# Second mixer's queries and maxima laid out by DMA, first mixer re-spaced

## The reference

```python
x = x + mixer_a(layernorm(x))   # linear attention, 32 heads of 4, two decays per head, rotary positions
x = x + ffn(layernorm(x))       # sum over 8 experts of (silu(x @ Wg) * (x @ Wu)) @ Wd, 128 -> 512 -> 128
x = x + mixer_b(layernorm(x))   # causal softmax attention, 16 query heads of 8, one key and one value head
x = x + ffn(layernorm(x))       # the same experts
```

## Time and profile before

| | |
|---|---|
| time, median of 3 runs | 1625.97 us (1619.76 to 1626.56) |
| profiled execution | 1626.03 us, span 1624.0 us |
| TensorE (PE) busy | 1496.0 us, 92% of the span |
| VectorE (DVE) busy | 1177.7 us, 73% |
| ScalarE (ACT) busy | 885.3 us, 55% |
| GpSimd (POOL) busy | 784.3 us, 48% |
| DMA | 216.28 MB, 133 GB/s over the span |
| granted TensorE clock | 0.976 of full speed |

### The profile page before, as it was taken

The page is one execution under the profiler, slowest core; times in us unless marked ns, Lnnn a source line. Parts: engine busy times, 40 slices in busy tenths (PEclk is TensorE's granted clock), DMA queues, the critical chain, the costliest instruction groups (busy, mean ns, idle before and its releaser), DMA issues. The chain is left out here.

```text
span 1624.0 us, 23328 instructions
## 1 busy us (share of the span) xinstructions
PE 1496.0 (92%) x7504; PEld 1111.4 (68%) x7504; DVE 1177.7 (73%) x1949; ACT 885.3 (55%) x1520; POOL 784.3 (48%) x732
## 2 busy tenths in 40 slices
PE   3478999899989899899999999999999999999998
PEld 2356777677776677577567676776767767677786
DVE  5678787869778787868677585775857758577565
ACT  2245556464554546444655557565575655755554
POOL 2537445543525244531315546555465554655565
PEclk8689999999999999999999999999999999999999
DMA  6125543434334343433332334333343333433352
GB/s 202 59 71 179 198 154 119 156 117 156 140 133 156 117 156 117 156 117 117 117 133 101 118 117 150 123 131 117 119 156 121 125 117 122 156 119 124 148 182 112
DMA packets 36380, 216.28 MB, mean 133 GB/s; under 512 B 3491, under 2 KB 17444, under 8 KB 19876
## 3 DMA queue, kind: packets, MB, share of 16 engines
q1 hardware_dynamic: 36260, 214.79, 36.5%
HBM read 200.10 MB, written 15.27 MB: 133 GB/s over the span
## 5 line engine op out<-in xcount | busy, mean ns | idle before, releaser
L531 POOL TENSOR_TENSOR HL<-HF,HH 128x512 fp32r<-128x512 f32 x312 | 416.0, 1333 | 476.4 <-ACT HH L705 475.3
L1215 DVE TENSOR_TENSOR HF<-SG,bank 128x512 f32<-128x512 f32 x512 | 350.4, 684 | 171.8 <-PE bank L874 92.1
L872 PE MATMUL bank<-XTH,W 128*128 128x512 f32 x1024 | 423.4, 413 | 10.4 <-ACT SG L698 9.9
L874 PE MATMUL bank<-XTH,W 128*128 128x512 f32 x1024 | 403.8, 394 | 0.0
L873 PE MATMUL bank<-XTL,W 128*128 128x512 f32 x1024 | 403.6, 394 | 0.0
L1198 DVE SCALAR_TENSOR_TENSOR SG<-SG,bank 128x512 f32<-128x512 f32 x288 | 197.3, 685 | 207.0 <-ACT SG L700 205.0
L700 ACT ACTIVATE SG<-bank 128x512 f32<-128x512 f32 x288 | 172.1, 597 | 318.0 <-PE bank L874 316.5
L705 ACT ACTIVATE HH<-HF 128x512 fp32r<-128x512 f32 x512 | 320.4, 626 | 37.6 <-DVE HF L1215 32.4
L698 ACT ACTIVATE SG<-bank 128x512 f32<-128x512 f32 x224 | 133.5, 596 | 251.7 <-PE bank L874 250.4
L872 PEld LDWEIGHTS bank<-XTH,W 128*128 128x128 f32 x1024 | 194.4, 190 | 82.3 <-issue 23.6
L872 PE MATMUL dbank<-HH,W 128*128 128x512 f32 x512 | 217.9, 426 | 16.1 <-DVE HL L1204 14.9
(11 more groups left out here) (212 smaller groups left out, 1796.7 us busy)
## 6 DMA issues: line engine op xcount, KB each, us to landing
W<-kept_w SPq DMA_DIRECT2D x120, 1536.0 KB, 6.3
kept_w<-W SPq DMA_DIRECT2D x8, 1536.0 KB, 6.2
X<-in_L_attn_a_x_dram SPq DMA_DIRECT2D x8, 256.0 KB, 5.7
WS<-in_L_ffn_Wg_dram SPq DMA_DIRECT2D x8, 256.0 KB, 6.4
WS<-in_L_ffn_Wu_dram SPq DMA_DIRECT2D x8, 256.0 KB, 6.7
WS<-in_L_ffn_Wd_dram SPq DMA_DIRECT2D x8, 256.0 KB, 6.5
out_dram<-X SPq DMA_DIRECT2D x8, 256.0 KB, 7.2
CST<-in_tables_dram SPq DMA_DIRECT2D x1, 834.0 KB, 6.4
```

The lines of the kernel that those rows point to most:

```text
L531: g.tensor_tensor(HL[:, n % HRING, :], HF[:, n % HFRING, :], HH[:, n % HRING, :].bitcast(F32), ALU.subtract).then_inc(F.hl, 1)
L872: pe.matmul(dst, wh, xh, start=start, stop=False)
L874: return pe.matmul(dst, wl, xh, start=False, stop=stop)
L1215: v.tensor_tensor(HF[:, n % HFRING, :], gated, fbank[(2 * n + 1) % 3], ALU.mult).then_inc(F.mul, 1)
```

## The change

Second mixer: the 0/1 matrices, `query_stack` and `stack2` go. SyncE stores QKH and QKL of the queries to HBM and loads them back spread over QST; VectorE splits the maxima into a small tile NMS, TensorE transposes it, ScalarE copies it (MT), SyncE stores it and loads it into the free partitions of QST. The maxima of a sequence are stored at r = 8 and 14 and spread at r = 9 and 15. `rows` then uses 24 of each 32 partitions, `cols` 26. The weight loads become part of a SyncE list by slots. Projections move three slots earlier, each of the column scores has its own slot, `exps` stands ahead of the gate's activation in its slot, and the buffer of exponentials is a ring.

First mixer: v2 and rep0 swap banks; Relu moves from ScalarE to GpSimd; the last two scans, the products that use them, the second numerators and all that follows come one slot later; in stages 0 to 5 the gate of unit 28 uses Tanh, as in the last stage, so that ScalarE keeps the table of Exp (`AHEAD`). `GAP` is 3 instead of 4, `B_LEAD` 35 instead of 36.

```diff
+AHEAD = [UNIT * s + 28 for s in range(NT - 2)]
-GAP = 4
+GAP = 3
-B_LEAD = 36
+B_LEAD = 35
...
-          "b1": (-6, 2, 2), "mx": (-5, 1, 0), "v0": (1, 1, 0), "den": (3, 2, 1), "v1": (4, 1, 0), "v2": (6, 0, 0),
-          "rep0": (6, 1, 1), "rep1": (7, 1, 2), "v3": (8, 1, 0), "z": (20, 2, 2), "fturn": (31, 1, 2)}
-NUM_POINT = ((13, 1), (17, 1))
+          "b1": (-6, 2, 2), "mx": (-5, 1, 0), "v0": (1, 1, 0), "den": (3, 2, 1), "v1": (4, 1, 0), "v2": (6, 0, 1),
+          "rep0": (6, 1, 0), "rep1": (7, 1, 2), "v3": (8, 1, 0), "z": (21, 2, 2), "fturn": (32, 1, 2)}
+NUM_POINT = ((13, 1), (18, 1))
+B_CELL = {"turn": (-17, 1, 3), "q": (-11, 2, 0), "qs": (-10, 1, 1), "k": (-10, 2, 2), "ks": (-9, 1, 0),
+          "v": (-8, 1, 1), ("mx", 0): (8, 1, 3), ("mx", 1): (14, 1, 3), ("pv", 0, 0): (17, 1, 3),
...
-COLS_AT = [[(12, 2), (14, 0), (15, 2), (17, 0)], [(18, 2), (20, 0), (21, 2), (23, 0)]]
+COLS_AT = [[(12, 2), (13, 2), (14, 2), (15, 2)], [(17, 2), (18, 2), (19, 2), (20, 2)]]
...
+            def spread_queries(t, part, src, done):
+                for g in range(NG):
+                    to = RG * g + DB * part
+                    rows = kept_q[src, RG * g:RG * (g + 1), :].rearrange("(j x) t -> x j t", j=NJ)
+                    sp.dma_start(QST[to:to + DB, :, :].bitcast(F32), rows).then_inc(done, 16)
+            def spread_maxima(n, b):
+                sp.wait_ge(B.mt_out, 32 * (n + 1))
+                rows = kept_m[b].rearrange("(r g j) t -> g r j t", r=2, g=NG)
+                for g in range(NG):
+                    to = RG * g + 3 * DB
+                    sp.dma_start(QST[to:to + 2, :, b * SEQ:(b + 1) * SEQ].bitcast(F32),
+                                 rows[g]).then_inc(B.mrow, 16)
+            def side_b(t, r):
+                if r == -8:
+                    sp.wait_ge(B.hi, 2 * t + 1)
+                    sp.dma_start(kept_q[0], QKH[:, 0, :].bitcast(F32)).then_inc(B.hi_out, 16)
+                if r == -7:
+                    sp.wait_ge(B.lo, 2 * t + 1)
+                    sp.dma_start(kept_q[1], QKL[:, 0, :].bitcast(F32)).then_inc(B.lo_out, 16)
+                    sp.wait_ge(B.hi_out, 16 * (t + 1))
+                    spread_queries(t, 0, 0, B.st_hi)
+                    spread_queries(t, 1, 0, B.st_hi)
+                if r == -6:
+                    sp.wait_ge(B.lo_out, 16 * (t + 1))
+                    spread_queries(t, 2, 1, B.st_lo)
...
+            for slot in range(0, G_LAST + 1):
+                for t, r in b_tiles(slot):
+                    side_b(t, r)
+                for x in range(NE, 2 * NT * NE):
+                    u = FC * (x - WRING + 1) - 1
+                    if slot == ffn_slot(u // UNIT) + u % UNIT + LAG + 1:
+                        load_weights(x)
...
+                if r in (-5, -3):                              # GpSimd, first mixer
+                    k = (r + 5) // 2
+                    g.wait_ge((A.u_k, A.u_q)[k], t + 1)
+                    g.tensor_scalar(R1[:, k, :], U[:, k, :], 0.0, None, ALU.max).then_inc(A.re, 1)
...
+            def gated_ahead(n):                                # VectorE
+                gated = SG[:, n % 2, :]
+                v.wait_ge(F.sil, n + 1)
+                v.scalar_tensor_tensor(gated, gated, 1.0, fbank[2 * n % 3], ALU.add,
+                                       ALU.mult).then_inc(F.mid, 1)
...
-                for (m, c), at in zip(SCANS, (0, 1, 3, 6, 8, 10, 12, 13, 14, 15)):
+                for (m, c), at in zip(SCANS, (0, 1, 3, 6, 8, 10, 12, 13, 15, 16)):
```

More of the change, by code:

```diff
@@ L308, in program @@
         Y = here("Y", u_at, TOK)
-        Z = here("Z", u_at + 4 * TOK, SUB, C)
-        ZN = here("ZN", u_at + 8 * TOK, SUB, C)
+        Z = take("Z", SUB, C)
+        ZN = take("ZN", SUB, C)
         PQ = take("PQ", TOK)
@@ L327, in program @@
         at["now"] = arena
-        NMP = take("NMP", 2, 2, NJ, P, dt=F32R)
+        NMS = take("NMS", 2, 64, dt=F32R)
+        MT = take("MT", 2, P, dt=F32R)
         VF = take("VF", SUB, RG)
         at["now"] = s_at
+        B1 = take("B1", 2, TOK)
+        B2 = take("B2", 2, TOK)
+        QK = take("QK", 2, TOK)
         QKH = take("QKH", 2, TOK, dt=F32R)
@@ L334, in program @@
         KST = take("KST", TOK, dt=F32R)
[L335 to L339, removed]
+        assert at["now"] <= r_at
+        PT = take("PT", 3 * PT_RING, TOK)
         OS = take("OS", 2, TOK)
@@ L355, in program @@
                       "rs ay y xb z zsum zg zb done")
-        B = sems("b", "proj roped u_q u_k hi lo v_ready v_used st_ready st_used kst_used row_ready row_used nmh nml "
-                      "q2_ready q2_used t_ready t_used t_cut pv os turn ro o ot otc out biased done")
-        F = sems("f", "gate up sil half mul hh hl hlv down ys back done")
+        B = sems("b", "proj roped u_q u_k hi lo v_ready v_used hi_out lo_out st_hi st_lo kst_used row_ready row_used nmh nml "
+                      "mx mt mt_out mrow t_ready t_used t_cut pv os turn ro o ot otc out biased done")
+        F = sems("f", "gate up sil half mul hh hl hlv down ys back done mid")
         stored = sem("stored")
@@ L393, in a_tiles @@
         def a_tiles(g):
-            return tiles(g, a_slot, -15, 32)
+            return tiles(g, a_slot, -15, 33)
         def b_tiles(g):
@@ L497, in _, with load_weights @@
             sp.dma_start(BRAW[:, C:], row(b_bk)).then_inc(ld.wb, 16)
-            for x in range(NE, 2 * NT * NE):
+            def load_weights(x):
                 sp.wait_ge(F.down, FC * (x - WRING + 1))
@@ new lines, in _ @@
+            for slot in range(0, G_LAST + 1):
[5 more added lines that the diff above has]
+                        load_weights(x)
+                        if x % NE == 4 and x // NE > NT:
+                            t = x // NE - NT - 1
+                            sp.wait_ge(F.done, NT + t + 1)
+                            sp.dma_start(o_tok[:, t], X[:, t, :, :]).then_inc(stored, 16)
@@ L696, in gate_act @@
                 after(act, F.mul, n - 1)
-                if n < TANH:
+                if n < TANH and n not in AHEAD:
                     act.activation(SG[:, n % 2, :], fbank[2 * n % 3], ACT.Silu).then_inc(F.sil, 1)
@@ L757, in side_a @@
                     act.activation(EX[:, :, :], U[:, :, :], ACT.Exp).then_inc(A.ex, 1)
-                if r == -2:
-                    act.wait_ge(A.ex, t + 1)
-                    act.activation(U[:, :, :], U[:, :, :], ACT.Relu).then_inc(A.re, 1)
                 if r in (7, 8):
@@ L810, in side_b @@
                             act.activation(OS[:, z, :], abank, ACT.Copy).then_inc(B.os, 1)
-                    for h in range(2):
-                        if r == B_CELL["stack", b, h][0]:
-                            act.wait_ge(B.q2_ready, 2 * n + h + 1)
-                            after(act, B.t_ready, 4 * (n - 1))
-                            act.activation(Q2[:, b, 2 * h:2 * h + 2, :], r3(sbank[bank_of(("b", t, ("stack", b, h)))], 2),
-                                           ACT.Copy).then_inc(B.q2_used, 1)
+                    if r == B_CELL["mx", b][0]:
+                        act.wait_ge(B.mx, n + 1)
+                        after(act, B.mt_out, 32 * (n - 1))
+                        act.activation(MT[0:64, b, :], sbank[bank_of(("b", t, ("mx", b)))][0:64, 0:P],
+                                       ACT.Copy).then_inc(B.mt, 1)
                     if r == B_CELL["ot", b][0]:
@@ L840, in _ @@
                 n = unit_of(slot)
-                if n is not None:
-                    gate_act(n)
+                if slot == b_slot(0):
+                    act.wait_ge(A.done, NT)
+                    act.wait_ge(A.z, NT)
                 for t, r in b_tiles(slot):
@@ L845, in _ @@
                         for i, (at, point) in enumerate(COLS_AT[b]):
-                            if r == at + (point == 2):
+                            if r == at + 1:
                                 exps(SPT * t + b, i)
+                if n is not None:
+                    gate_act(n)
                 n = unit_of(slot - 1)
@@ L996, in rows @@
                     pe.wait_ge(B.kst_used, t + 1)
-                    pe.wait_ge(B.st_used, NJ * (t + 1))
-                q = [QST[g * RG:(g + 1) * RG, :, b * SEQ:(b + 1) * SEQ] for g in range(NG)]
-                ks = [KST[g * RG:(g + 1) * RG, b * SEQ:(b + 1) * SEQ] for g in range(NG)]
+                    pe.wait_ge(B.st_hi, 8 * 16 * (t + 1))
+                    pe.wait_ge(B.st_lo, 4 * 16 * (t + 1))
+                q = [QST[g * RG:g * RG + 3 * DB, :, b * SEQ:(b + 1) * SEQ] for g in range(NG)]
+                ks = [KST[g * RG:g * RG + 3 * DB, b * SEQ:(b + 1) * SEQ] for g in range(NG)]
                 masks(i)
@@ L1056, in project_out, with turn_maxima @@
                 m.then_inc(B.out, 1)
-            def stack2(n, b, h, bk):
-                pe.wait_ge(B.nml, 2 * (n + 1))
-                for x in range(2):
-                    j = 2 * h + x
-                    dst = bk[:, x * SEQ:(x + 1) * SEQ]
```

(11 more changed lines are left out.)

210 lines of the change are left out of this document (96 added, 114 removed), and 2 rows, old and new, of the table B_CELL.

## The result

The changed kernel takes **1647.69 us** (median of 3 runs, 1646.55 to 1647.89) against 1625.97: a ratio of 1.0143 [1.0105, 1.0182]: 1.4% slower, clear of 1. Its profiled execution has a span of 1646.0 us (1624.0 before).

The account below looks back on a forecast made before the run. TensorE was taken as the bound: its work in the second mixer, its waits in the first. Second mixer -14, gap -1 and first mixer -25 gave -40 us from 1626.03, so 1586 us, range 1556 to 1652.

Parts of the forecast that it names:

- I take the issue rate: Second mixer, SyncE queue: twelve spreads priced at 0.46 us each, giving a weight wait of about 2 us per tile, 17 in eight.
- the stated range: Whole kernel: 1556 to 1652 us, from 13 us below the second rival up to the lower half of the first.
- first rival: Second mixer: narrow spreads take 1.1 us each, weight wait 10.9 us per tile, 1657 us, clock may fall too; chance 0.26.
- the forecast's own: Whole kernel: the range around 1586 us without the narrow-spreads rival, 1563 to 1610 us; chance of the forecast 0.42.
- its open point: Second mixer: whether 64 KB spreads into 8 partitions run at the issue rate, as loads into 128 partitions did.
- TensorE work removed, transposes, exponentials, gap: Second mixer: products removed -36 us, transposes added +3, exponentials' re-spacing +2.4, one slot less between the phases -1.
- Maxima: Second mixer, maxima stored and spread by SyncE: no wait expected, up to 2 us per tile if one link is late.
- (a) bank swap: First mixer: v2 follows the denominators instead of VectorE's keyed v1; 5.8 us of waits falls to 1.2, -4.6.
- (b) scans: First mixer: later scans and numerators cut 20.2 us of waits for GpSimd's products and low halves, -11.7.
- (c) tail: First mixer, end of tile: Relu on GpSimd and Tanh gate, -0.6 us in waits, and -3 from half clock avoided.
- nothing won: First mixer, tail: waits of 0.9, 1.0 and 0.6 us expected where there were 1.4 and 1.2; -0.6 in all.
- (d) before 200 us: Start of kernel: the same first-mixer waits as tiles 0 and 1 pass alone, -5 us, 1 of it from Relu's place.

Follow-up runs that it names:

- the best version: Changed kernel with the query spreads issued behind the weight load and into every third partition, keys' weights, biases and rotary tables matched: 1567.69 us, ratio 0.9656 against the kernel before.
- the old spacing: Version with queries laid out by TensorE (1580.09 us), with the last two scans, their products and the second numerators one slot earlier, as before: 1589.71 us.
- the old tail: Version with queries laid out by TensorE (1580.09 us), with Relu back on ScalarE and no Tanh gate ahead of the last stage: 1579.46 us.

## Why the prediction was wrong

The step that failed is the price of the twelve spreads: "I take the issue rate". They were issued at that rate, but took 1.06 us each to run, and the load behind them ran late. The wait was 69.4 us in seven tiles instead of 17 in eight. The half clock after it, which only the rival named, cost about 16 (the 81 us between this kernel and the best version from the sixth point on, less 65 of waits; an estimate). The measured time lies inside the stated range only because that reached into the first rival; the forecast's own ended at 1610. The first rival had the mechanism, the 1.1 us and the 10.9 us (9.9 measured). That its 1657 us came as near as it did to 1647.7 is partly luck: it counted 87 us of waits, in eight tiles, and left the clock out of its sum. The argument that decided for the issue rate, 64 KB loads landing in 2 us when issued 0.44 us apart, came from loads into 128 partitions. The prediction named that as its open point and left it at a chance of 0.26, with the rule that it cites from the Trainium skill, page "SBUF — State Buffer", section "Door 1: The DMA port swizzle", against it and no row for it; it should have been the likelier case.

The other steps, one by one:

- *TensorE work removed, transposes, exponentials, gap:* -31.6 us forecast. From the sixth point on, the best version takes 936.4 us against 968.3, 31.9 less; but 5.0 of that fall in the next stage, which still holds the first mixer's last tile (and a wait of 3.9 for weights), so 26.9 are the second mixer's alone. A steady stage became 3.5 us shorter, where the forecast's terms come to 3.8. The exponentials cost 5.7 us, not 2.4.
- *Maxima:* no wait forecast, 0.3 us found.
- *(a) bank swap:* 4.6 forecast, 0.85 per stage, some 5 in six. Right.
- *(b) scans:* 11.7 forecast; 1.2 per stage for the scans alone, 7 in six, and up to 1 per stage more if what is left belongs to the later tail. Of the two waits in this term only the one for low halves went, which the old spacing brings back (7.8 us in five stages). The one for GpSimd's products, forecast at about 1 us per tile, is 1.5 where it was 1.3, and only the last tile's fell, to 2.8.
- *(c) tail:* 0.6 forecast, 0.9 per stage measured. The waits for the gate and XNF, 7.1 and 5.4 us in five stages with the old tail, are 4.0 and 3.9 without it; "nothing won" was wrong. The half clock had cost about 4 us where 3 were forecast.
- *(d) before 200 us:* 5 forecast, 3 measured, within the spread of that point.

Up to the sixth point, so without its last tile, the first mixer gave 27 us where 25 were forecast for all of it. The loss came from the spreads: with them behind the load and in other partitions, the rest of the change makes the kernel 57 us faster than before, not 22 slower.

## What to carry to other kernels

A transfer's cost on the queue is how long it runs, not how long its issue takes, and a row of a transfer with another layout does not price it: when the layout is new, the cheap case needs its own row. Here the narrow transfers belonged behind the wide load that was due next, and into partitions that do not lie together; either alone left the stage at 105 us, both gave 97.7. A second issuing queue did not shield the load, which landed after 11 to 13 us instead of 6.3. A wait of ten microseconds on TensorE cost some two more in clock.

## What the runs showed that was not expected

The issue of a spread into every third partition takes 0.70 us, into neighbours 0.40: the faster transfer has the slower issue, and these issues, 8.4 us in all, kept half the wait where the spreads stood ahead of the load. Twice as many transfers of half the size took as long as before, and those with four times longer runs in HBM too. The spacing of the scans took away the wait for low halves and left the one for GpSimd's products much as it was.
